# A cross-attention and expert kernel: value matmuls ahead of the projection, two transposes behind the next round's scores, and VectorE's steps to match

## What is computed

```python
def reference(x, ctx_1024, ...):
    # x: (16, 256, 256), ctx: (16, 77, 256), 16 heads of 16
    x = x + xattn(layernorm(x), ctx)      # q from x, k and v from ctx, softmax over 77 keys, @ Wp + bp
    x = x + ffn(layernorm(x))             # 8 experts, top 2 of a router
    return x

def ffn(x):
    xf = layernorm(x) * g + b
    scores, idx = top_k(xf @ router_w, 2)
    gate = softmax(scores)
    # per expert: layernorm, (x @ W1 + b1) * silu(clip(x @ W2 + b2)), clip, @ Wo + bo, clip
    return sum(gate[e] * expert_e(xf) for e in chosen)
```

## Time and profile before

| | us |
|---|---|
| median of 3 runs | 973.76 |
| lowest and highest | 971.99, 973.82 |
| the profiled execution | 973.42 |
| its span, first to last instruction | 971.6 |
| end of the attention rounds, about | 370 |
| TensorE busy in the span | 911.0 |
| VectorE, ScalarE, GpSimd busy | 746.9, 659.2, 408.1 |

### The profile page before, as it was taken

The page is one execution under the profiler, slowest core; times in us unless marked ns, Lnnn a source line. Parts: engine busy times, 40 slices in busy tenths (PEclk is TensorE's granted clock), DMA queues, the critical chain, the costliest instruction groups (busy, mean ns, idle before and its releaser), DMA issues.

```text
span 971.6 us, 19262 instructions
## 1 busy us (share of the span) xinstructions
PE 911.0 (94%) x6200; PEld 812.3 (84%) x6200; DVE 746.9 (77%) x1763; ACT 659.2 (68%) x1336; POOL 408.1 (42%) x649
## 2 busy tenths in 40 slices
PE   5999999999998898899999999999999999999973
PEld 4778878888877786788999989898998998989973
DVE  2778777777788697877888888886877877869862
ACT  3667776767667584666777777867776767677841
POOL 3554675776668646311423140505124143051232
PEclk9999999999989899999999999999999999999997
DMA  6322322332246344734555555826817657267332
GB/s 142 57 61 52 82 68 68 82 90 67 60 100 199 101 165 161 202 123 126 161 143 169 161 142 172 234 88 180 305 24 231 231 141 251 94 180 217 95 68 24
DMA packets 132624, 129.16 MB, mean 133 GB/s; under 512 B 59984, under 2 KB 117408, under 8 KB 132384
## 3 DMA queue, kind: packets, MB, share of 16 engines
q1 hardware_dynamic: 119648, 110.36, 37.6%
q0 software_dynamic: 12864, 17.44, 9.8%
HBM read 102.01 MB, written 25.36 MB: 131 GB/s over the span
## 4 chain that ended last, share of the span: by engine, by line
PE 76%; issue 7%; ACT 6%; DVE 6%; another core or an unknown queue 2%; POOL 2%; DMA 1%; SPq 0%; ACTq 0%; POOLq 0%; DVEq 0%
PE bank L1909 33%; PE bank L1953 16%; PE bank L1769 5%; PE bank L1709 4%; PE bank L1691 3%; PE bank L1901 3%; PE bank L1746 2%; PE bank L1736 2%; PE bank L1792 2%; PE bank L1941 1%; PE bank L1797 1%; PE bank L1878 1%; PE bank L1805 1%; PE bank L1781 1%
## 5 line engine op out<-in xcount | busy, mean ns | idle before, releaser
L841 POOL DMA_INDIRECT out_rows<-yo,token x68 | 113.7, 1672 | 400.3 <-ACT yo L1089 338.6
L1909 PE MATMUL bank<-xh,wh 128*128 128x512 f32 (+1 forms) x672 | 236.3, 352 | 13.4 <-DVE gate_in L1573 7.2
L1909 PE MATMUL bank<-xl,wh 128*128 128x512 f32 (+1 forms) x672 | 230.1, 342 | 3.6 <-issue 3.6
L1909 PE MATMUL bank<-xh,wl 128*128 128x512 f32 (+1 forms) x672 | 229.7, 342 | 0.1
L1549 DVE TENSOR_TENSOR wl<-raw,wh 128x1024 fp32r<-128x1024 f32 x126 | 152.4, 1220 | 25.9 <-ACT wh L1020 24.7
L1909 PEld LDWEIGHTS bank<-xh,wh 128*128 128x128 f32 x672 | 129.1, 192 | 28.5 <-DVE gate_in L1573 10.2
L1953 PE MATMUL bank<-wh,hh 128*128 128x256 f32 x512 | 146.3, 286 | 1.1 <-DVE yo L1608 1.1
L1953 PE MATMUL bank<-wl,hh 128*128 128x256 f32 x512 | 144.8, 283 | 0.9 <-issue 0.9
L1953 PE MATMUL bank<-wh,hl 128*128 128x256 f32 x512 | 144.9, 283 | 0.0
L1909 PEld LDWEIGHTS bank<-xh,wl 128*128 128x128 f32 x672 | 128.8, 192 | 19.2 <-issue 4.2
L1909 PEld LDWEIGHTS bank<-xl,wh 128*128 128x128 f32 x672 | 129.2, 192 | 11.4 <-issue 0.5
(11 more groups left out here) (188 smaller groups left out, 1878.3 us busy)
## 6 DMA issues: line engine op xcount, KB each, us to landing
raw<-in_W SPq DMA_DIRECT2D x42, 1024.0 KB
raw<-in_Wo SPq DMA_DIRECT2D x25, 1024.0 KB
whole<-in_W SPq DMA_DIRECT2D x8, 1024.0 KB, 6.3
xs<-in_x SPq DMA_DIRECT2D x32, 128.0 KB, 2.3
out_rows<-x SPq DMA_DIRECT2D x32, 128.0 KB, 1.8
shared<-z_rows SPq DMA_DIRECT2D x7, 520.0 KB
bo_row<-in_bo SPq DMA_DIRECT2D x25, 128.0 KB
k_blocks<-k_parts SPq DMA_DIRECT2D x128, 19.2 KB
```

Of the source, the lines that this page charges most:

```text
L841: e.indirect_dma_start(out=out, out_offset=bass.IndirectOffsetOnAxis(ap=token[j % 4][:, s:s + 1], axis=0), in_=yo[j % 2][:, s, :], in_offs ...
L1909: mm = e.matmul(ps[:, h * cols:(h + 1) * cols], ws[split_before(j) % 2][:, w, c, m * P:(m + 1) * P], xx[j % 2][:, c, 0:cols], start=(h == ...
```

## The change

On TensorE, `values(i - 1)` comes ahead of `project(i - 2)` and `place_pair`. `transpose_xn` and `transpose_xf` leave the end of the round and stand behind the first scores of the next round; for the last rounds (i of 30 and more, and the first ones, i below -1) they stay at the end. The bank turns stay as they were, since the order of the users of banks 6 and 7 doesn't change. On VectorE, the low parts of keys or queries, `x_sums` and `normalized` come ahead of `make_x1`. SyncE's, GpSimd's and ScalarE's programs are untouched.

```diff
--- before.py
+++ after.py
@@ -1515,24 +1515,24 @@
                     early_table()
                 if 0 <= i - 4 < NT:
                     xf_variance(i - 4)
+                if 0 < nb < BATCH and even:
+                    low_keys(nb)
+                if batch and not even:
+                    low_queries(nb)
+                if 0 <= i + 5 < NT:
+                    x_sums(i + 5)
+                if 0 <= i - 1 < NT:
+                    normalized(i - 1)
                 if 0 <= i - 2 < NT:
                     make_x1(i - 2)
                 if even and 0 <= i // 2 - 4 < PAIRS:
                     find_slots(i // 2 - 4)
-                if 0 < nb < BATCH and even:
-                    low_keys(nb)
-                if batch and not even:
-                    low_queries(nb)
                 if 0 <= i - 2 < NT:
                     x1_sums(i - 2)
                 if 0 <= i + 5 < NT:
-                    x_sums(i + 5)
+                    x_variance(i + 5)
                 if 0 <= i - 2 < NT:
                     x1_variance(i - 2)
-                if 0 <= i + 5 < NT:
-                    x_variance(i + 5)
-                if 0 <= i - 1 < NT:
-                    normalized(i - 1)
                 if 0 <= i - 6 < NT:
                     best_experts(i - 6)
                 p = (i - 7) // 2
@@ -1821,11 +1821,22 @@
                          cum[:, 2 * p:2 * p + 3, :].rearrange("p t x -> p (t x)"), start=False,
                          stop=True, skip_group_check=True).then_inc(place_mm, 1)
 
+            def behind_scores(i):
+                return 0 <= i + 1 < NT - 1
+
+            def transpose_rows_of_blocks(i):
+                if 0 <= i + 3 < NT:
+                    transpose_xn(i + 3)
+                if 0 <= i - 4 < NT:
+                    transpose_xf(i - 4)
+
             def round_first(i):
                 even, nb = i % 2 == 0, i // 2 + 1
                 batch = 0 <= nb < BATCH
                 if 0 <= i < NT:
                     scores(i, 0)
+                if behind_scores(i - 1):
+                    transpose_rows_of_blocks(i - 1)
                 if 0 <= i - 1 < NT:
                     transpose_probs(i - 1, 0)
                 if 0 <= i - 2 < NT:
@@ -1844,20 +1855,18 @@
                     transpose_probs(i - 1, 2)
                 if 0 <= i - 5 < NT:
                     route_logits(i - 5)
+                if 0 <= i - 1 < NT:
+                    values(i - 1)
                 if 0 <= i - 2 < NT:
                     project(i - 2)
                 if i % 2 == 0 and 0 <= i // 2 - 4 < PAIRS:
                     place_pair(i // 2 - 4)
-                if 0 <= i - 1 < NT:
-                    values(i - 1)
 
             def round_third(i):
                 if i % 2 and 0 <= i // 2 + 2 < BATCH:
                     transpose_ctx(i // 2 + 2)
-                if 0 <= i + 3 < NT:
-                    transpose_xn(i + 3)
-                if 0 <= i - 4 < NT:
-                    transpose_xf(i - 4)
+                if not behind_scores(i):
+                    transpose_rows_of_blocks(i)
                 if i == NT - 2:
                     transpose_rows(0, (0, 1))
```

## The result

| | before | after |
|---|---|---|
| median, us | 973.61 (968.19 to 973.82, 5 runs) | 999.72 (996.36 to 1004.12, 5 runs) |
| profiled execution, us | 973.42 | 1004.12 |
| its span, us | 971.6 | 1002.3 |
| mean granted clock | 0.973 | 0.959 |

The changed kernel takes 1.0267 times as long, 95% interval 1.0234 to 1.0301: 26 us slower. The forecast was 977.3, with 989 as the upper end.

What follows compares the result with a forecast made beforehand. Early attention pairs were taken as bound by TensorE's own order (17.55 us), afterwards by a closed loop of 18.42 through x1 and SyncE. 973.4 + 4.1 (rounds 2 to 10) + 1.0 (10 to 28) - 1.2 (late rounds) = 977.3 us; range 967 to 989.

Steps and rivals of the forecast that it cites:

- x1 2.8 us later: Every attention round: with project behind transposes and values, VectorE's x1 starts at +8.79 instead of +6.00.
- x1 to v_blocks 10.9 to 12.7: Sign of being right: the distance from x1 through SyncE's queue to GpSimd's v_blocks stays at 10.9 to 12.7 us.
- The loop closes: Pairs of rounds: x1, SyncE's loads, v_blocks, y, probs_t, values, project and x1 again form a loop that sets pair length.
- The loop's length, 18.42: Once around: 10.92 + 3.52 + 2.32 + 0.06 + 0.45 + 1.15 = 18.42 us, longer than TensorE's 17.55.
- The fall: Rounds 10 to 28: granted clock dropping to 1.2 GHz, 1.69 us each, taken in one pair of four, adding 0.42.
- +4.1 for rounds 2 to 10: Four early pairs: the loop needs 4 x 18.42 = 73.68 us where they took 69.54, so +4.1 us.
- Late release and 1.5 us for x1: Odd rounds, 10 to 28: x1 released late behind GpSimd's indirect writes, so normalized-row transposes wait 1.5 us for it.
- The rule of the Trainium skill that was weighed: Against late release: engine and DMA ports are disjoint, so lateness need not follow the writes; time would be 972.1.
- Nine later pairs, +1.0: Rounds 10 to 28: TensorE's 17.55 + 1.5 + 0.42 for falls makes 19.5 us against 19.37, nine times 0.1.
- -1.2 in the late rounds: Late round at 332.25: project's 1.24 us wait for attn_t gets the value matmuls as cover, -1.2 us.
- The gaps of 0.54 us for c_t: Ends of odd rounds, six pairs: final-row transposes, moved 0.62 us later, no longer wait 0.54 us for ScalarE's context copy.
- The rival of falls in every pair, 988.6: Rounds 10 to 28: clock falls in all nine pairs, 20.74 us each, +12.3; 988.6 in all, chance 0.18.

Runs made afterwards that it cites:

- second trace of this kernel: The changed kernel itself, unedited, run once more on the third chip (kernel before: 961.6 us): 999.23 us, ratio 1.0391.
- last kernel: Kernel before with moved transposes, x1's store behind the key copies, and the first nine pairs' indirect writes in odd rounds: 969.67 us, ratio 1.0005.
- all edits: Changed kernel with x1's store behind key copies, routing scores behind values, route table behind first subtraction, first nine pairs' indirect writes in odd rounds: 983.12 us, ratio 1.0131.
- both edits: Changed kernel with SyncE's store of x1 behind the key copies and the routing scores behind the values: 972.14 us, ratio 1.0105.

## Why the prediction was wrong

- **x1 2.8 us later: right.** In the round from 83.65 project starts at +7.57 and x1 at +8.71; +7.64 and +8.79 were worked out.
- **x1 to v_blocks 10.9 to 12.7: right**, 10.7 to 12.2. ScalarE's y waits for shift, as forecast.
- **The loop closes: right**, and shown for rounds 2 to 10 by moving SyncE's store. In the first early pair TensorE also waits where I said, inside the values for probs_t:

```profile
62.35 0.64 PE L1769 MATMUL bank<-v_blocks,probs_t 128*128 128x34 f32 x4 [1.44 <-ACT probs_t L945]
...
79.91 0.61 PE L1781 MATMUL bank<-router,xf_t 128*128 128x8 f32 x4 [0.66 <-ACT k_t L899]
```

- **The loop's length, 18.42: the step that failed.** The term from y on was "2.32 + 0.06 + 0.45 + 1.15", 3.98 us, which lets the values start early and takes only their last two blocks into the loop. In the first pair (19.15 us), where no routing scores exist yet, it is 4.31, and the 0.3 more are a clock fall in project. From round 5 on the routing scores stand ahead of the values and claim the bank that ScalarE's k_t reads. In the second pair (19.47 us, the row at 79.91) it is 1.08 us from y (78.83) to them and 3.85 from there to x1 (83.76): 4.93 in place of 3.98, with no fall behind y. I had left the keys' copies out as "behind y in its queue" without asking what on TensorE waits for them.
- **The fall: priced outside the loop.** I counted falls in rounds 10 to 28 only, in one pair of four. They came in the early pairs too, and stretched values and project, which are links of the loop: 7.5 us from y instead of 4.9, and 22.73 for the third pair; 5.9 and 20.53 for the fourth. I had argued that a fall eats up the idle that brings the next; behind y the loop has no idle that a fall could eat.
- **+4.1 for rounds 2 to 10: +12.3** (81.88 against 69.54). Of the 8.2 us beyond the forecast 2.9 are the routing scores (0.95 in three pairs), 3.8 the falls behind y, and 1.8 the way from x1 to v_blocks, which I took from one distance (10.92) where the four are 11.1 to 11.8; the way from v_blocks to y was 0.3 shorter.
- **Late release and 1.5 us for x1: right** (1.73 us at 219.84; 0.9 to 2.0 in seven odd rounds). The rule of the Trainium skill that was weighed (SBUF — State Buffer, "SBUF: two separate sides") has ScalarE never wait at its ports. The runs show ScalarE's logits late with VectorE's x1 all the same (156.69, 3.77 us of idle), and the lateness follows the writes. Whether it arises at a port or in how a semaphore is seen, no run separates. On two chips it is absent: the order of work alone does not set it.
- **Nine later pairs, +1.0: +7.4** (184.71 against 177.32 us, from x1 of round 10 to that of round 28). The pair itself was nearly right: 19.44 us in the only one without a fall and 20.8 to 21.0 in the five with one, where 19.05 and 20.74 were forecast. Mis-sized was how often: "a fall in one pair of four" was eight of nine. VectorE's tail behind x1, set at "0 to 0.3 us a pair, which the loop's idle takes in", shows in no wait of TensorE in these pairs; in the second trace of this kernel, where x1 is prompt, waits of 0.4 to 1.1 us for probs are in most of them.
- **-1.2 in the late rounds: +5.3** in two pairs (44.01 against 38.71 us). The -1.2 had no ground: the wait for attn_t at 332.25 is that of round 33, and there are no values left in that round to cover it (the last, of tile 31, start at 325.02). It is still there in the changed kernel:

```profile
361.24 1.10 PE L1746 MATMUL bank<-wp,attn_t 128*128 128x256 f32 x4 [1.23 <-ACT attn_t L952]
```

  The rest of the 5.3 was not looked into by a run of its own.
- **The gaps of 0.54 us for c_t: gone, as forecast**, but not the falls that followed them.
- **The first x1**: 5.6 us later. The 2.8 us that the prediction worked out for every x1 have no term in its sum, though nothing behind the last x1 gave them back. The first x1 lies between 39.6 and 42.8 us in the seven traces with TensorE's and VectorE's orders of before (transposes moved or not), so part of the rest is scatter; what is left is open.

These add up: 5.6 + 12.3 + 7.4 + 5.3 = 30.6 of the 30.7 us between the spans. The rival of falls in every pair, 988.6, came nearest: it had the later pairs nearly right, and the same loop term.

## What to carry to other kernels

When a step moves, follow what hangs on its result through every queue until it comes back. If it comes back, each link counts at full length, and so do the steps that stand between two links on the same engine, with every buffer that they claim. Here a closed loop a few per cent longer than the bounding engine's own work cost more than the difference, since clock falls lay in links of the loop, where nothing covers them. Opening one loop can leave a second one standing right behind it: compare the distances again after each edit, in every stretch. And work that used to lie under another engine's long step (here VectorE's under the values) is on the path as soon as its input comes behind that step.

## What the runs showed of the hardware

- **Chips differ in how VectorE and ScalarE are let go behind GpSimd's indirect writes.** On two chips x1 came 0.04 to 0.15 us behind project in rounds 11 to 25, on the three others and that of the result up to 1.5 to 2.3 us behind it in some of the rounds 11 to 26. The kernel before takes 962 and 963 us on the former, 969 to 975 on the latter. That the late release makes this difference is a guess that the last kernel did not bear out. Part of it lies elsewhere: behind the last x1, in the expert tiles, the changed kernel takes 639.9 us on the chip of the result and 635.6 on the third.
- **The clock falls with TensorE not seen idle.** With all edits (fifth chip) TensorE is busy in all of 40 to 110 us, as far as the profile shows (it models when a matmul ends, so short pauses can be hidden), and yet from 75 us on the clock goes to its lower level once in each round, each time while project runs, behind the values and the routing scores. Stretches of that kernel:

```profile
40.00:110.00 70.00, 70.00 (x497) 59.38 (x497) 51.33 (x165) 45.08 (x117) 35.03 (x79) 0.90 0.28 54
```

```profile
84.00:86.00 2.00, 2.00 (x13) 1.79 (x13) 1.30 (x4) 0.96 (x3) 2.00 (x6) 0.79 0.01 4
86.00:88.00 2.00, 2.00 (x11) 1.31 (x10) 1.25 (x7) 0.60 (x2) 0.09 (x2) 0.50 0.01 2
```

  The kernel with both edits has the same order of TensorE and 1.00 in the same stretch, on the third chip. The Trainium skill (TensorE: Matmul & The Clock Gate, "Part 1: The HAM clock gate (the "warmup" mystery)") ties the lower level to an idle engine; this trace shows no idle for it. In seven traces of kernels with TensorE's and VectorE's orders of before (transposes moved or not) there was no fall from 40 to 110 us, and none either in the changed kernel with VectorE's order undone, which idles 6.35 us in that stretch. What sets the fall off stays open.
